# A two-layer attention kernel on one core: a new planner for the side work between attention steps, with projections in halves

## The reference, cut to what matters

```python
# x: 4 sequences of 1024 tokens, 128 channels, fp32
x = layernorm(x + proj(softmax(l2norm(q) @ l2norm(k) / temperature / 8) @ v))     # layer 0, 16 heads of 8, all keys
x = layernorm(x + int8_matmul(quantized(x)) + bias)
x = layernorm(x + Wo(softmax(causal(rope(ln(q)) @ rope(ln(k)) / sqrt(8))) @ v))   # layer 1, causal
x = layernorm(x + down(silu(gate(x)) * up(x)))                                    # 384 hidden
```

## Time and profile before

| | before |
|---|---|
| median of 3 runs | 832.14 us (831.68 to 834.26) |
| profiled execution, its time | 833.45 us |
| profiled execution, its span | 831.4 us |
| mean granted TensorE clock | 0.993 |
| exps, first start to last end | 20.24 to 806.7 us |
| TensorE units in slots | 202, of them 15 projections |
| slots in FRONT, BETWEEN | 84, 37 |

### The profile page before, as it was taken

How to read it: one execution, slowest core, us unless ns; L and a number is a source line. 1 busy time by engine, 2 the same in 40 slices (tenths; PEclk the granted TensorE clock), 3 DMA queues, 4 the chain that set the end, 5 groups by cost and what they waited for, 6 DMA issues and landing times.

```text
span 831.4 us, 18912 instructions
## 1 busy us (share of the span) xinstructions
PE 803.6 (97%) x7457; PEld 295.6 (36%) x7457; DVE 540.3 (65%) x1426; ACT 772.3 (93%) x869; POOL 169.9 (20%) x370
## 2 busy tenths in 40 slices
PE   8899999999999999999999999999999999999996
PEld 4223332333333433343333433343333343443444
DVE  4265666868867787876663677675754267785656
ACT  4899999999999999999999999999999999898972
POOL 3110000100000601033000611023200354362220
PEclk9899999999999999999999999999999999999999
DMA  5765414242602631362130421321231231071000
GB/s 144 248 225 190 177 40 146 83 141 76 242 27 88 231 140 39 99 232 78 59 133 26 150 81 39 140 90 45 72 130 51 81 110 51 27 240 53 15 14 15
DMA packets 48556, 88.74 MB, mean 107 GB/s; under 512 B 5200, under 2 KB 14544, under 8 KB 48464
## 3 DMA queue, kind: packets, MB, share of 16 engines
q1 hardware_dynamic: 47696, 85.95, 30.4%
q0 software_dynamic: 288, 1.05, 0.4%
q10 hardware_dynamic: 480, 0.48, 0.2%
HBM read 50.50 MB, written 35.65 MB: 104 GB/s over the span
## 4 chain that ended last, share of the span: by engine, by line
PE 75%; ACT 13%; DVE 7%; issue 3%; DMA 0%; ACTq 0%; DVEq 0%
PE ps L1011 37%; PE ps L989 21%; ACT probs L826 13%; PE ps L879 9%; PE ps L868 3%; PE ps L964 3%; DVE th L1421 1%; DVE hT L1422 1%; PE ps L873 1%; PE ps L1045 1%; PE ps L1053 0%; DVE sums_t L1249 0%; DVE gate_sb L1416 0%; DVE mid_part L1411 0%; DVE mid_part L1412 0%
## 5 line engine op out<-in xcount | busy, mean ns | idle before, releaser
L826 ACT ACTIVATE probs<-ps 128x1024 f32<-128x1024 f32 x800 | 749.3, 1057 | 31.0 <-PE ps L989 21.2
L1011 PE MATMUL ps<-probs,v_st 128*32 128x512 f32 (+3 forms) x3584 | 428.1, 560 | 3.2 <-issue 2.4
L989 PE MATMUL ps<-q_st,k_st 32*128 32x512 f32 (+3 forms) x1792 | 266.3, 460 | 7.8 <-ACT probs L826 7.2
L989 PEld LDWEIGHTS ps<-q_st,k_st 32*128 32x128 f32 x1792 | 120.1, 182 | 288.0 <-ACT probs L826 221.7
L734 POOL TENSOR_SCALAR_AFFINE_SELECT probs<-probs 128x256 f32<-128x256 f32 x256 | 103.8, 428 | 144.7 <-ACT probs L826 143.0
L1011 PEld LDWEIGHTS ps<-probs,v_st 128*32 128x32 f32 x3584 | 78.7, 108 | 110.4 <-issue 74.2
L702 POOL COPY v_st<-v_all 128x256 f32<-128x256 f32 (+1 forms) x65 | 29.1, 456 | 343.2 <-PE ps L1011 334.9
L1249 DVE STREAM_TRANSPOSE sums_t<-ps 128x512 f32<-128x512 f32 x32 | 22.9, 716 | 45.3 <-PE ps L1011 44.7
L1390 DVE COPY mid_qkv<-ps 128x384 f32<-128x384 f32 x32 | 17.8, 557 | 35.8 <-PE ps L879 34.8
L964 PE MATMUL ps<-yTp,w_hid 128*128 128x512 f32 x84 | 31.2, 453 | 4.1 <-DVE gate_sb L1416 2.5
L1390 DVE COPY prep_qkv<-ps 128x384 f32<-128x384 f32 x24 | 13.4, 558 | 27.1 <-PE ps L879 26.4
(11 more groups left out here) (190 smaller groups left out, 641.3 us busy)
## 6 DMA issues: line engine op xcount, KB each, us to landing
k_st<-parts_scratch SPq DMA_DIRECT2D x46, 512.0 KB, 3.6
parts_scratch<-mid_part SPq DMA_DIRECT2D x34, 512.0 KB, 4.4
q_st<-parts_scratch SPq DMA_DIRECT2D x62, 256.0 KB, 3.9
parts_scratch<-prep_part SPq DMA_DIRECT2D x28, 512.0 KB, 4.8
k_st<-parts_scratch SPq DMA_DIRECT2D x17, 256.0 KB, 2.9
xT<-in_xT SPq DMA_DIRECT2D x8, 256.0 KB, 4.4
x_all<-in_x SPq DMA_DIRECT2D x8, 256.0 KB, 5.3
out<-yo SPq DMA_DIRECT2D x7, 256.0 KB, 2.3
```

The lines of the kernel that those rows point to most:

```text
L826: nc.scalar.activation(probs[:, k % PS, :, 0:w], slot(k)[:, :, 0:w], ACT.Exp).then_inc(probs_ready, 1)
L989: last_ = mm(slot(k)[:, e, at:at + n], k_st[row, p % KB, kt * P:(kt + 1) * P], q_st[row, p % KB, lo:HALF], start=True, stop=not shifted)
L1011: last_ = mm(acc[HR * h:HR * (h + 1), lo:HALF], v_st[:, p % VB, kt, h, :], probs[:, (2 * s + h // 2) % PS, h % 2, at:at + n], start=FIRST[ ...
```

## The change

New constants of durations, taken from VectorE's and TensorE's records; a new model of the loop (`Course`: scores at the time that a PSUM pair is free, exps 0.903 us apart, sums 0.955 us), with which each slot is tried with sums behind, in front and between, with and without each running job's next unit. A unit that is not late is taken where it holds ScalarE up by at most `EASY` = 0.25 us, a late one up to `HURRY` = 2.0 us; from slot `TAIL` = 322 all count as late. Jobs start 6 slots after their chunk's last step (4 before) and are due 9 slots (4 before) ahead of the first use. A projection is two units of two tiles, 4 and 5 slots after the last step, each with its own read on VectorE. In `CHUNKS` each layer-1 chunk of the first four moves one place ahead. `FIRST_KEYS`' second qkT goes from slot 1 to slot 5. After each of the scores k = 3 to 6 two zero products are written to bank `ACC`.

```diff
-CHUNKS = [(0, 0), (0, 1), (0, 2), (0, 3), (1, 0), (0, 4), (1, 1), (0, 5),
-          (1, 2), (0, 6), (1, 3), (0, 7), (1, 4), (1, 5), (1, 6), (1, 7)]
+CHUNKS = [(0, 0), (0, 1), (0, 2), (1, 0), (0, 3), (1, 1), (0, 4), (1, 2), (0, 5), (1, 3), (0, 6), (0, 7),
+          (1, 4), (1, 5), (1, 6), (1, 7)]
...
-PE_US = {"qkT": 0.6, "normT": 0.6, "qkv": 0.9, "proj": 1.15, "xqT": 0.4, "ffn": 0.4, "gate": 0.7, "up": 0.7, "down": 0.95}
+PE_US = {"qkT": 0.6, "normT": 0.6, "qkv": 0.66, "proj": 0.45, "xqT": 0.34, "ffn": 0.34, "gate": 0.67, "up": 0.67, "down": 0.66}
+READ_US = {"qkT": 1.5, "normT": 0.75, "qkv": 0.6, "proj": 0.45, "xqT": 0.5, "ffn": 1.45, "gate": 0.75, "up": 1.45, "down": 0.35}
+DVE_US = {"ln_stats": 1.25, "ln_aggr": 1.0, "ln_out": 1.6, "ln_out_x": 1.55, "ln_out_y": 1.75, "amax": 1.2, "quant": 1.55,
...
+EXP, EXP_DONE, SCORED, TANH, PAIRS, SPLIT, MASK = 0.903, 1.1, 0.545, 0.46, 0.427, 0.19, 0.95
...
+def sums_us(s):
+    return 0.955 + 0.04 * (len(STEPS[s][1]) - 1)
...
+OVER, TURN_BY, FREE, ROWS_BY = 1.9, 2.6, 3, 9
+PACE, DVE_PACE, HURRY, EASY, WAIT, LATE_WAIT, PROJECT, URGE, TAIL, WITHIN = 1.0, 0.4, 2.0, 0.25, -0.25, 3, 4, 0, 322, 36
+class Course:
...
+    def exp(self, at, tanh=0):
+        self.act.append(max(self.act[-1] + EXP + TANH * tanh if self.act else 0.0, at + SCORED))
+        self.done.append(self.act[-1] + EXP_DONE)
+        self.k += 1
+    def free(self):
+        return self.done[-SLOTS] if self.k >= SLOTS else 0.0
+    def scores(self, both, tanh=0):
+        at = max(self.pe, self.free())
+        self.exp(at, tanh)
+        if both:
+            two = self.free()
+            at = at if two <= at else max(at + SPLIT, two)
+            self.exp(at)
+        self.pe = at + PAIRS
+    def stall(self):
+        return max(0.0, max(self.pe, self.free()) + SCORED - self.act[-1] - EXP)
...
     for c in range(NCH):
-        after = LAST_STEP[passes_of(0, c)[-1]] + 4
-        jobs.append(dict(name="mid", c=c, after=after, due=min(first_slot(passes_of(1, c)[0]) - 4, after + 28)))
+        after = LAST_STEP[passes_of(0, c)[-1]] + PROJECT + 2
+        due = first_slot(passes_of(1, c)[0]) - ROWS_BY
+        if c < NCH - 1:
+            due = min(due, LAST_STEP[passes_of(0, c + 1)[-1]] + 2)
...
-    out[1] += FIRST_KEYS[1:]
+    out[1] += FIRST_KEYS[1:2]
+    out[5] += FIRST_KEYS[2:]
...
+        orders = ["behind"]
+        if s >= 2 and not ends_pair(step):
+            orders = ["behind"] if not s <= NS - FREE else ["behind", "front"]
+            if BRANCHED <= s < NS - 2:
+                orders.append("between")
+        if pending:
+            orders = ["front"]
...
+        if projected:
+            (plain, at, _), order = best(orders, "proj", bank)
+            out[s].append((None, projected[0], "pe", "proj", projected[1]))
+            dve = bank = max(dve, at + 0.15) + READ_US["proj"]
+        elif 2 <= s <= NS - FREE:
+            base = plain.stall() + plain.act[-1]
+            for j in live:
...
+                (got, at, _), o = best(orders, what, by)
+                extra = got.stall() + got.act[-1] - base
+                late = s + steps_left(j) - j["due"] if s < TAIL else 1.0
+                if extra > (HURRY if late > 0 else EASY) or by > plain.pe + (LATE_WAIT if late > 0 else WAIT):
+                    continue
...
-                for t in range(TC):
+                for t in range(2 * k, 2 * k + 2):
                     last_ = quarters(side[:, t * P:(t + 1) * P], attn[:, t * P:(t + 1) * P], w_out[:, layer, :])
...
+                    if k < WARM[4]:
+                        keep_warm(2, ACC)
...
-                tt(x, side_t, x, ALU.add).then_inc(side_read, 1)
+                x = x_all[:, b * NH2 + qh, tiles(k), :]
+                tt(x, side_t[:, tiles(k), :], x, ALU.add).then_inc(side_read, 1)
```

More of the change, by code:

```diff
@@ L198, in side_order @@
     out[0] += FIRST_KEYS[:1]
-    out[1] += FIRST_KEYS[1:]
+    out[1] += FIRST_KEYS[1:2]
+    out[5] += FIRST_KEYS[2:]
     turns = [LAST_STEP[p] + 1 for p in range(1, NP, 2)]
-    pe = act = dve = bank = turned = 0.0
-    scores_at = [0.0, 0.0]
-    for s in range(NS + 1):
[L204 to L215, removed]
+    dve = bank = turned = 0.0
@@ new lines, in side_order, with steps_left, slot, sums @@
+    now = Course()
+    now.scores(True)
+    now.scores(False)
+    def steps_left(j):
+        units = UNITS[j["name"]][j["n"]:]
+        return sum(PACE if e == "pe" else dve_us(what, 0) * DVE_PACE for e, what, k in units)
+    for s in range(NS + 1):
+        tanh = sum(x[3] == "gate" for x in out[s - TANH_AT]) if s >= TANH_AT else 0
+        step = s - 1
+        pending = s > 1 and STEPS[step][4] and STEPS[step][0] % 2 == 0
+        summed = [0.0]
+        def slot(order, unit=None, ready=0.0):
+            c, at = now.copy(), 0.0
+            more = s < NS - 1
+            def sums():
+                c.pe = max(c.pe, sums_from, turned if pending else 0.0) + sums_us(step)
+                summed[0] = c.pe
+            sums_from = c.done[-4] if s and len(c.done) >= 4 else 0.0
+            if s and STEPS[step][3]:
+                sums_from += MASK
+            if order == "between":
+                c.scores(False, tanh)
+                sums()
+                c.scores(False)
+            elif more:
+                c.scores(True, tanh) if 2 * s + 4 < 2 * NS else c.scores(False, tanh)
+            if order == "behind" and s:
+                sums()
+            if unit:
+                c.pe = max(c.pe, ready) + PE_US[unit]
+                at = c.pe
+            if order == "front" and s:
+                sums()
+            return c, at, summed[0]
+        def best(orders, unit=None, ready=0.0):
+            found = [(slot(o, unit, ready), o) for o in orders]
+            return min(found, key=lambda x: (round(x[0][0].stall() + x[0][0].act[-1], 2), x[0][0].pe))
@@ L281, in side_order @@
+        now = plain
+        if order == "front":
+            front.add(s)
+        elif order == "between":
+            between.add(s)
+        end = now.pe + (TURN_BY if s + 1 in turns else 9.0)
         for j in live:
@@ L521, in program @@
     POOL_CONSTS = 11
-    WARM = (10, 4, 0, 22)
+    WARM = (10, 4, 0, 22, 7)
     NLATE = 9
```

125 lines of the change are left out of this document (53 added, 72 removed).

## The result

The changed kernel takes **838.3 us** (median of 7 runs, 836.96 to 841.83); the kernel before took 833.1 us in 7 runs, and between 831.8 and 832.5 us in each of the larger sets that follow. The ratio is 1.0072, 95% interval 1.0056 to 1.0087: **slower by 0.7%**, where 817.1 us and faster was forecast. The profiled execution took 838.42 us, 4.97 above that of before.

What follows compares the result with a forecast made beforehand. ScalarE was taken as the bound, losing 51.0 us. Terms 3.2 + 4.1 + 3.2 + 2.1 + 0.7 + 3.1 - 0.5 - 0.9 = 15.0 us, off the 832.14 us median, gave 817.1; range 807 to 829.

Steps and rivals of the forecast that it cites:

- Head: Slots 0 to 6: zero products and the later second qkT keep TensorE's clock up; gain 3.2 us, bounds 0 and 3.5.
- What the move drags along ... Cost nothing: Second qkT to slot 5: VectorE's read and SyncE's store of chunk 1's q move too, with slack; cost nothing.
- Projections, 4.1 in the middle: Slots 7 to 339: projections in halves hold TensorE 0.50 us each instead of 0.99; 4.1 us gained.
- 15 more slots: Projection halves take 15 more slots from units, at 0.03 us each: 0.5 us against.
- 0.7 for the tail's halves: Tail, slots 340 to 399: projections in halves cut 0.86 us of lateness to 0.1; 0.7 us gained.
- Better run starts, 3.2: Runs of units stay, but each of 16 starts better under the planner, 0.2 us each: 3.2 us, bounds 0 and 16.9.
- Between: Sums put into TensorE's wait between two scores: a run's first unit costs 0 instead of about 0.07 us.
- VectorE's true durations, 2.1: Middle: measured VectorE durations stop TensorE being sent to unready results; half of 4.2 us, 2.1 gained, bounds 0 and 4.2.
- No wait is added: Layer 1 one chunk closer: its first chunk wants rows at slot 96 instead of 128, there long before; no added wait.
- Tail, 3.1: From slot 322: true durations halve some 6.2 us of waits in six slots; 3.1 us gained, bounds -3 and 6.2.
- Rival D: Slots 340 to 399: units taken before their data under the 2.0 us licence cost about 1.0 each; slower; chance 0.07.
- Work left for the end, 0.9: End: one or two down products, four out rows and a LayerNorm may be left; 0.9 us against, bounds 0 and 2.5.

Runs made afterwards that it cites:

- rows and end mended: Changed kernel with VectorE's branch and GpSimd's v copy moved, tail licence from slot 310, last chunks' projections 3 slots behind: 827.28 us, ratio 0.9928.

## Why the prediction was wrong

The sum had eight terms. What each did:

- **Head, 3.2: right.** 2.7 us by the zero products alone, 3.6 with the qkT moved and the branch ahead of its read. But "What the move drags along ... Cost nothing" failed. It followed SyncE's store and left out what stands behind that read on VectorE, the branch: 4.2 us in the medians, 3.0 in its slots. This was the first gap, and the trace of before has it: 4.4 us between VectorE's branch and its next instruction.
- **Projections, 4.1 in the middle: mis-sized.** 2.0 us (5.4 to 3.4 in the changed kernel, 1.9 alone). The price of "15 more slots", 0.5, was too low: alone they made 8 more run slots, 2.3 us. The 0.7 for the tail's halves was not measured by itself.
- **Better run starts, 3.2: about the size, by another way.** Run slots fell from 63 to 50, their loss from 16.4 to 13.3. "Between" was hardly used (5 slots, 37 before), so the mechanism that the sum named did not act.
- **VectorE's true durations, 2.1: not seen.** Slots over 0.33 in that stretch lost 8.4 us before and 9.6 after. Only with the v copy moved do they fall to 6.4. The step that failed is that the only wait looked at was TensorE for VectorE. The plan has nothing of GpSimd's queue, only a constant of 0.95 us for a step's masks (`MASK`, new): the queue of masks, v copies and bias additions comes out by slots, and each new plan lands differently on it. That was 3.7 us here, 6 us in slots 132 to 134 with the old order, with the fall of the clock there.
- **"No wait is added" by the order of chunks: right for mid 0, false for the kernel.** The new order alone costs 3.3 us. And mid 7's rows, which the prediction did not follow, came late: its last qkT has 6 slots ahead of its pass, and had 9.
- **Tail, 3.1: wrong in sign.** 15.9 us lost before, 19.4 after, 4.4 of that behind the late rows. Without them slots 322 to 399 still lose 0.7 (this kernel) to 2.4 us (rows and end mended) more than before. Rival D named this stretch, but by units taken under the licence of 2.0 us and at a price of 1.0 each, and gave it 0.07. TensorE's waits for hT (4.1 us in five of over 0.35) are of that kind; how much of them is due to the licence was not tried, since without it (or at 1.0 us) the units don't fit ahead of the end.
- **Work left for the end, 0.9: mis-sized.** It was 2.4; the bound of 2.5 held.

Added from the trace: the head gains 3.3 us and first exps come 0.4 earlier; the middle loses 2.8 more, the tail 3.5 more, the end 2.4 more: 5.0 in all, the difference of the two profiled executions. By runs: branch 4.2, v copy 3.7, rows and end 3.1, together 11.0 us. These are differences of medians, and the cost of point 4 differs between executions, so each is rough (the branch's own slots give 3.0). Without the three the same plan stands at 827.3, 4.5 us below the kernel before in its own set (6.0 by the ratio), a third of the 15 that were forecast, and 3.6 of that is the head. The 0.88 for faster was given to a plan whose gains were read off, but whose new collisions were not looked for: each of its moves put a known instruction in a new place in some queue, and three of them were dear.

## What to carry to other kernels

When an order is computed again, the gain is the small part: go through every queue that the model lacks (here GpSimd's, SyncE's and VectorE's one branch), and list what now stands ahead of something that the bounding engine waits for. A gap in an idle engine's trace, such as 4.4 us behind a branch, is a price that a moved instruction can bring due. And a planner's slack must be tested as a whole: with the units further apart, the runs got 5 us cheaper and the kernel 9 us slower.

## What the hardware showed

- A mask on GpSimd (0.40 us alone) beside a VectorE piece with two SBUF inputs ends 0.27 us behind it, even where that makes 1.40 us (325.80 to 327.20, beside L1293 to 326.93) or 0.85 (327.51 to 328.36, beside L1380 to 328.10); beside VectorE's copy from PSUM and its reduction it takes 0.40. The Trainium skill, "SBUF — State Buffer", section "SBUF: two separate sides", states this as an exclusive lock on a shared port pair, the loser blocked for the whole instruction; the rows agree.
- VectorE's branch: about 1 us of loads ahead of it, and 4.4 to 4.6 us from its end to the next instruction. It is free where the engine idles anyway (in the run with the branch moved it ends at 24.26 us, nine ahead of the next work).
- TensorE's clock fell to 0.5 around waits of 2.8 to 7.8 us (from 41.1, 746.3 and 526.2 us on in three kernels), but not around the 2.83 us at 41 us in the changed kernel; in the kernel before it fell at 23.6 us with no wait over 0.42 us since 20 us. It stayed there 6.8 or 10.2 us in these, and 3.4 us behind the 2.18 us at 328.9 in the changed kernel. The same kind of wait does not always do it: behind the branch, 2.84 us came with a fall and 2.83 without. The 2.90 us for late rows cost the exps 4.4, and 1.42 us for the same rows without a fall 1.0.
